# Decoder on one core: the second attention's values products issued for two key tiles at a time, with three buffers of exponentials

## The reference, cut to what matters

```python
q = latents @ w_q.T                      # 2048 x 256
kv = x @ w_kv.T                          # 1601 keys
k, v = jnp.split(kv, 2, axis=-1)
attn = jnp.einsum('blhd,bshd->bhls', q, k) * SCALE
attn = jax.nn.softmax(attn, axis=-1)
out = jnp.einsum('bhls,bshd->blhd', attn, v)
return out.reshape(B, L, DIM) @ w_out.T + b_out
```

## Time and profile before

| | us |
|---|---|
| median of 3 runs | 2223.26 |
| lowest, highest run | 2219.47, 2227.24 |
| the profiled execution's own time | 2219.07 |
| its span, first to last instruction | 2217.00 |
| PE busy | 1857.7 (84%) |
| DVE busy | 1084.9 (49%) |
| ACT busy | 932.1 (42%) |
| units of the second attention, from 1043 to 1681 | 638 |

### The profile page before, as it was taken

How to read it: one execution, slowest core, us unless ns; L and a number is a source line. 1 busy time by engine, 2 the same in 40 slices (tenths; PEclk the granted TensorE clock), 3 DMA queues, 4 the chain that set the end, 5 groups by cost and what they waited for, 6 DMA issues and landing times.

```text
span 2217.0 us, 27165 instructions
## 1 busy us (share of the span) xinstructions
PE 1857.7 (84%) x7552; PEld 797.6 (36%) x7553; DVE 1084.9 (49%) x1481; ACT 932.1 (42%) x1663; POOL 262.7 (12%) x215
## 2 busy tenths in 40 slices
PE   6789969999799685848999999999996369999980
PEld 2334422332244232313333333333322346666650
DVE  4663258776211324439887688788741212111215
ACT  3331236677411424232777677577684012211210
POOL 4143010000200202120000000000002410000005
PEclk9999979999899797977999999999998589999995
DMA  9101051100100002280000000000003510000003
GB/s 332 34 31 46 0 118 30 30 27 11 54 0 0 5 0 25 22 144 22 8 16 9 9 16 8 9 15 8 2 1 162 215 46 24 28 28 28 26 26 111
DMA packets 64088, 95.78 MB, mean 43 GB/s; under 512 B 11504, under 2 KB 56752, under 8 KB 62074
## 3 DMA queue, kind: packets, MB, share of 16 engines
q1 hardware_dynamic: 60922, 86.21, 13.4%
q0 software_dynamic: 3072, 8.39, 1.2%
HBM read 65.20 MB, written 28.97 MB: 42 GB/s over the span
## 4 chain that ended last, share of the span: by engine, by line
PE 55%; DVE 5%; issue 5%; POOL 3%; ACT 3%; DMA 1%; SPq 0%; DVEq 0%; ACTq 0%; POOLq 0%
PE ps L517 9%; PE ps L1793 9%; PE ps L1148 8%; PE ps L1170 8%; PE ps L1107 8%; PE ps L1808 5%; DVE arena L1302 2%; PE ps L1450 2%; PE ps L1205 1%; POOL rows_in L1902 1%; PE ps L441 1%; POOL arena L1907 1%; PE ps L1801 1%; DMA qparts<-arena 1%; ACT arena L1861 1%
## 5 line engine op out<-in xcount | busy, mean ns | idle before, releaser
L1251 ACT ACTIVATE arena<-ps 128x512 f32<-128x512 f32 x1088 | 575.1, 600 | 242.9 <-PE ps L1170 241.4
L1302 DVE TENSOR_REDUCE arena<-ps 128x1 f32<-128x802 f32 (+1 forms) x512 | 480.6, 985 | 106.2 <-PE ps L1107 104.9
L517 PE MATMUL ps<-arena 128*128 (+1 forms) x832 | 383.0, 621 | 73.6 <-DVE arena L1591 23.2
L1107 PE MATMUL ps<-arena 97*128 97x401 bf16 (+2 forms) x1280 | 347.9, 354 | 47.8 <-DVE arena L1302 18.1
L1170 PE MATMUL ps<-arena 100*128 100x512 bf16 x1088 | 370.2, 385 | 10.0 <-ACT arena L1251 5.2
L1148 PE MATMUL ps<-arena 128*32 128x512 f32 x2176 | 289.8, 605 | 1.4 <-ACT arena L1251 1.4
L517 PEld LDWEIGHTS ps<-arena 128*128 128x128 f32 x832 | 164.3, 199 | 291.2 <-issue 291.2
L1793 PE MATMUL ps<-arena 128*128 x608 | 198.8, 470 | 29.3 <-ACT arena L1861 29.3
L1107 PEld LDWEIGHTS ps<-arena 97*128 97x128 bf16 x1280 | 114.1, 99 | 237.4 <-DVE arena L1302 109.3
L1170 PEld LDWEIGHTS ps<-arena 100*128 100x128 bf16 x1088 | 104.9, 98 | 260.4 <-ACT arena L1251 186.5
L1988 DVE TENSOR_TENSOR arena<-ps,arena 128x352 f32<-128x352 f32 x76 | 40.0, 526 | 269.4 <-ACT arena L1868 197.3
(11 more groups left out here) (187 smaller groups left out, 1451.4 us busy)
## 6 DMA issues: line engine op xcount, KB each, us to landing
arena<-in_experts_w SPq DMA_DIRECT2D x8, 2176.0 KB, 16.9
arena<-qparts SPq DMA_DIRECT2D x192, 64.0 KB, 2.3
qparts<-arena SPq DMA_DIRECT2D x48, 128.0 KB, 2.0
rows_in<-arena SPq DMA_DIRECT2D x1, 5120.0 KB, 35.5
arena<-in_ctxT SPq DMA_DIRECT2D x3, 1664.0 KB, 9.6
kparts<-arena SPq DMA_DIRECT2D x24, 208.0 KB, 2.4
arena<-kparts SPq DMA_DIRECT2D x12, 416.0 KB, 14.6
arena<-rows_in SPq DMA_DIRECT2D x38, 128.0 KB, 2.0
```

The source lines that it names most:

```text
L517: ins = eng.matmul(out, w[:, k, m * P:(m + 1) * P], x[:, k, tok(c)], start=k == 0, stop=k == ktiles - 1)
L1107: ins = eng.matmul(slot_banks(s_static)[:, x, 0:n_keys], Qst[0:97, ring, heads[x], q * P:(q + 1) * P], Kst[0:97, at_head(ring * HG + heads ...
L1251: eng.activation(probs[:, keys_of(u, kt) % 2, h, :], ring_bank(r), ACT.Exp, bias=0.0).then_inc(ring_read.sem, 1)
L1302: eng.tensor_reduce(MX[:, par, heads[0] * QT + q, n % 2:n % 2 + 1], got, AX.XY, ALU.max).then_inc(slot_free.sem, 1)
```

## The change

In the second attention alone (`a` is 1), an odd key tile issues no block any more, and an even key tile `kt` from 2 on issues two, those of key tiles `kt - 2` and `kt - 1`, one right behind the other (`values_at`). Key tile 0 issues the block of key tile 12 of the unit before, as it did. A unit so has 6 double blocks and one single one where it had 13 single ones. The wait in front of a double block is for the exponentials of its second key tile. The exponentials go round three buffers (`exps`, `exps_of`): `probs`, and 2048 words of the area that the feed-forward weights had; the first exponential of a key tile waits for the block of three key tiles before (`exps_free_after`). The order of scores and items in `KEY_TILE` is not touched, nor are the ring of 3 banks and the 2 slots. The first attention's plan stays as it is.

```diff
--- before.py
+++ after.py
@@ -836,6 +836,7 @@
                         2: (0, "item", 1, 2, "item", 3, "pv"), 3: ("item", 0, "item", 1, 2, 3, "item", "pv")}
             AT_DEN, AT_TURN, AT_OUT = (1, 1, 3) if window else (2, 8, 11)
             Kst = Kst_narrow if window else Kst_wide
+            exps = [probs[:, 0, :, :], probs[:, 1, :, :], f32(ffn_at + 512, HG, CH)][0:2 + a]
             ctx_w, Vaug_w = ctxT[:, :, 0:keys], Vaug[:, 0:n_kt, :, :]
 
             def at_head(h):
@@ -974,17 +975,40 @@
                     eng.wait_ge(window_steps, WINDOW_STEPS + 1)
 
 
+            def values_at(kt):
+
+                if kt == 0:
+                    return (n_kt - 1,)
+                if a == 0:
+                    return (kt - 1,)
+                if kt % 2 == 0:
+                    return (kt - 2, kt - 1)
+                return (kt - 1,) if kt == n_kt - 1 else ()
+
+            def exps_of(u, kt):
+                return exps[(u % 2 + kt) % 3 if a else (n_kt * u + kt) % 2]
+
+            def exps_free_after(u, kt):
+
+                if kt >= 2 + a:
+                    return kt - 1 - a
+                if u == 0:
+                    return None
+                if a == 0:
+                    return kt - 1
+                return max(t for t in range(n_kt) if (u - 1) % 2 + t - u % 2 - kt in range(-30, 31, 3)) + 1 - n_kt
+
             def plan(u):
 
                 items = [(1, n) for n in range(AHEAD, PAIRS)] if u <= 6 else []
                 items += [(2, n) for n in range(AHEAD)] if u <= 5 else []
                 for kt in range(n_kt):
                     mine = items[PAIRS * kt // n_kt:PAIRS * (kt + 1) // n_kt]
-                    values = (kt - 1, 0) if kt else (n_kt - 1, -1)
+                    group = values_at(kt)
                     for place in KEY_TILE[len(mine)]:
                         if place == "pv":
-                            if kt > 0 or u > 0:
-                                yield ("pv",) + values
+                            if group and (kt > 0 or u > 0):
+                                yield ("pv", group, 0 if kt else -1)
                         elif place == "item":
                             yield ("item",) + mine.pop(0)
                         else:
@@ -1146,7 +1170,7 @@
                 def values(w, kt):
                     for h in range(HG):
                         ins = eng.matmul(o_bank[32 * h:32 * h + 32, :], Vaug[:, kt, (w % 4) * HG + h, :],
-                                         probs[:, keys_of(w, kt) % 2, h, :], start=kt == 0, stop=kt == n_kt - 1,
+                                         exps_of(w, kt)[:, h, :], start=kt == 0, stop=kt == n_kt - 1,
                                          skip_group_check=True)
                     ins.then_inc(pv_done.sem, 1)
 
@@ -1170,14 +1194,15 @@
                             eng.matmul(ring_bank(r), Kst[0:ROWS, at_head(g * HG + h), kt * P:(kt + 1) * P],
                                        Qst[0:ROWS, g, h, :], start=True, stop=True).then_inc(ring_full.sem, 1)
                         elif what == "pv":
-                            _, kt, before = step
+                            _, group, before = step
                             if before:
                                 ring_read.wait(eng, ring_before(i))
                             else:
-                                ring_read.wait(eng, ring_before(i) + (ring_place(u, ("scores", kt, HG - 1)) + 1))
-                            if kt == 0 and u > 0:
+                                ring_read.wait(eng, ring_before(i) + (ring_place(u, ("scores", group[-1], HG - 1)) + 1))
+                            if group[0] == 0 and u > 0:
                                 o_copied.wait(eng, i)
-                            values(u + before, kt)
+                            for kt in group:
+                                values(u + before, kt)
                         elif what == "item":
                             _, ahead, n = step
                             v = u + ahead
@@ -1246,9 +1271,9 @@
                             _, kt, h = step
                             r = ring_place(u, step)
                             ring_full.wait(eng, ring_before(i) + (r + 1))
-                            if h == 0 and (u > 0 or kt >= 2):
-                                pv_done.wait(eng, n_kt * i + kt - 1)
-                            eng.activation(probs[:, keys_of(u, kt) % 2, h, :], ring_bank(r), ACT.Exp,
+                            if h == 0 and exps_free_after(u, kt) is not None:
+                                pv_done.wait(eng, n_kt * i + exps_free_after(u, kt))
+                            eng.activation(exps_of(u, kt)[:, h, :], ring_bank(r), ACT.Exp,
                                            bias=0.0).then_inc(ring_read.sem, 1)
                             if to_invert is not None:
                                 invert(u, i, to_invert)
@@ -1256,7 +1281,7 @@
                         elif step[0] == "den":
                             to_invert = ring_place(u, step)
                             log_den(u, i, to_invert)
-                        elif step == ("pv", n_kt - 1, -1):
+                        elif step == ("pv", (n_kt - 1,), -1):
                             copy_o(u, i)
                     assert to_invert is None
```

## The result

| | us |
|---|---|
| median of 4 runs, the change | 2252.70 (2248.59 to 2254.73) |
| median of 4 runs, before | 2225.25 (2219.47 to 2227.99) |
| ratio to before | 1.0124, 95% interval 1.0098 to 1.0151 |
| the profiled execution's own time, its span | 2254.73, 2252.8 |

The account below looks back on a forecast made before the run. PE was taken to set the pace, with items waiting for DVE's slots after double blocks: +2.14 us a unit, 16 units +34, on 2219.1 gives 2253, plus 4.2 for the median: 2257 us, range 2237 to 2280.

Parts of the forecast that it names:

- The saving: PE, second attention: 13 blocks per unit become 7, so 96 x 0.19 = 18 us less PE work in 16 units.
- a way in and out: PE going into and out of a block standing alone: about 0.19 us lost, 0.09 going in and 0.10 going out.
- The joint: Place inside a double block where its second tile follows the first: taken to cost nothing, at most 0.19 us.
- The walk: Two regular key tiles stepped through from the first score behind a double block: 6.05 us instead of 5.82, +0.23.
- Item c: Third item after a double block: could start at 1.57 us, needs the first item's slot until 1.82, waits 0.25.
- d: Fourth item after a double block: could start at 2.39 us, needs the second item's slot until 2.72, waits 0.33.
- The unit: Whole unit of the second attention, summed over its key tiles: +2.14 us, in 16 units +34 us.
- the negation: DVE work between two reduces, key tiles 6 to 8: about 0.35 us with waits; that stretch +0.53.
- item e: Fifth item after a double block: at 3.72 us without waiting for its slot; 0.3 later between key tiles 6 and 8.
- The last two units: Last unit, without items, and the one before: +2.1 us each, with -1.1 as the other end.
- The gain: Rival: DVE never holds items up, so each unit loses 1.1 us, 18 in all: 2205 us; chance 0.08.
- The dear joint: Rival: joining two blocks costs a full way out and in, or weight loads show: up to 18 us more, 2275; chance 0.12.

## Why the prediction was right

It forecast 2257 us and a loss of 34; measured are 2252.7 and 27 (the forecast added to a median of 2223.3; the one measured beside the change is 2225.25). The mechanism and its places are as walked:

- *The saving.* 0.19 for a way in and out was right: 5.83 becomes 5.64 where no item waits for its slot. The joint costs nothing. A double block takes 1.86, 0.04 less than priced. The second tile's eight weight loads come in two fours, and each four begins with the round before its own (PE's second round, then PEld):

```profile
1316.01 0.61 PE L1172 MATMUL ps<-arena 128*32 128x512 f32 x4
1315.55 0.16 PEld L1172 LDWEIGHTS ps<-arena 128*32 128x32 f32 x8 [0.34 <-ACT arena L1276]
1316.01 0.13 PEld L1172 LDWEIGHTS ps<-arena 128*32 128x32 f32 x4 [0.30 <-issue]
1316.44 0.13 PEld L1172 LDWEIGHTS ps<-arena 128*32 128x32 f32 x4 [0.30 <-issue]
```

  The sentence of the Trainium skill about weight loads and rows ("TensorE: Matmul & The Clock Gate", Part 3, The mechanism) does not hold as it stands for these blocks: fours of loads, 0.13 us each four and on the same rows, pass under matmuls in flight. The paragraph above that sentence names the background weight buffer as a second case; no run here shows whether that is the cause.
- *The walk.* Item c was to wait 0.25 and waits 0.47 - 0.22 = 0.25; d was to wait 0.33 and waits 0.55 - 0.22 = 0.33; two key tiles were to take 6.05 and take 6.02.
- *The unit.* Predicted and measured: key tiles 2 to 4, 4 to 6, 10 to 12 at +0.69 and +0.60; 6 to 8 at +0.53 and +0.32; 8 to 10 at +0.53 and +0.46; 12 to 0 at +0.90 and +0.85; 0 to 2 at -0.51 and -0.50. Sum +2.14 and +1.73. Of the 0.41 too much, 0.24 is the double block, six times 1.90 where it takes 1.86. The largest error in one place, 0.17, is the negation between key tiles 6 and 8, taken at 0.35 us of DVE; it held item e up by 0.13 where 0.30 was walked.
- *The last two units.* Taken at +2.1 each, as one end of two; they took +2.1 and +2.5, where the ring sets the pace. That both came so near is in part luck, since these units were not walked.
- *The rivals.* The gain is there when reduces are halved: a block that stands alone costs 0.19 more, but with full reduces that was not what bounded the pair of key tiles. The Trainium skill has it that changing the tiling mode drains TensorE ("TensorEngine Tiling", Key Properties). The 0.19 agrees with that. The dear joint didn't show, and c and d wait 0.58 together, well above the 0.22 at which gain and loss would cancel.

Left open: finer slots (four of one bank instead of two of two), which might feed DVE across a double block, were not tried.

## What to carry to other kernels

In this kernel, grouping work of one kind on the engine that sets the pace saved its changeovers, but it made a silence for every engine that it feeds, and those engines can bridge only what their buffers hold. Before grouping, lay the silence (here 1.86 us) beside the buffers in hand (two slots of 0.90 us each, the second filled late) and the time until the first new result arrives: a mean load of 72% hid that DVE's work no longer fitted in between. A few steps walked with start-to-start prices gave 6.05 where 6.02 was measured.

## What had not been expected of the hardware and the kernel

The way from the first item to the first score shrank by 9.7 us with halved reduces. There DVE sets the pace for much of the time, though in the units it doesn't but for key tiles 8 to 10: its reduces take 41.1 of the 59.3 us before, with 2.4 us of idle time in front of them. And of all kernels run, the fastest doesn't group anything: finding the maxima over half of the keys with single blocks takes 2156 us, 3% less than before. The subtracted number cancels in the softmax; what is given up is the guard against a score among the other keys that is larger than the maximum by so much that its exponential overflows, so whether that may be done is a question of the inputs and not of the profile.
